# Attention with FP4-scaled weights on one core: where the weight loads stand in SyncE's queue, and where GpSimd's weight steps stand in a slot

## The reference

```
x = x + layernorm(attention(layernorm(x)))     # 16 heads of 128
x = x + layernorm(ffn(layernorm(x)))           # 8 experts, top 2
attention: w = codes * repeat(scales, 32, axis=0)   for wq, wk, wv (256 x 2048) and wo (2048 x 256)
           q, k, v = x @ w + b ; softmax(q k^T / sqrt(128)) v ; @ wo + bo
ffn:       softmax router, top-2 experts, silu(x Wg) * (x Wu) @ Wd, combined
```

## Time and profile before

| | |
|---|---|
| median of 3 runs | 2091.43 us |
| the profiled execution's own time | 2085.26 us |
| its span in the profile | 2083.5 us |
| TensorE matmul busy | 1966.5 us (94%) |
| VectorE busy | 1750.0 us (84%) |
| GpSimd busy | 1525.5 us (73%) |
| ScalarE busy | 1417.0 us (68%) |
| attention, roughly | 30 to 1850 us of the span |

### The profile page before, as it was taken

One profiled execution on the slowest core, in us unless ns is written; L12 is line 12 of the kernel. 1 busy time (PEld: TensorE's weight loads), 2 busy tenths in 40 slices (PEclk: granted clock), 3 DMA queues, 4 the chain that ended last, 5 costly groups with the idle time before them and its releaser, 6 DMA issues.

```text
span 2083.5 us, 33186 instructions
## 1 busy us (share of the span) xinstructions
PE 1966.5 (94%) x10902; PEld 1697.1 (81%) x10902; DVE 1750.0 (84%) x2706; ACT 1417.0 (68%) x2686; POOL 1525.5 (73%) x1317
## 2 busy tenths in 40 slices
PE   6999999999999999999999999999999999976882
PEld 5888888888888888888888888888888888865772
DVE  7889889998989888988999898988898898976444
ACT  5777767776777767776777667776777667762444
POOL 2679778887778777977888777977787787973222
PEclk9999999999999999999999999999999999986996
DMA  4667757786767767775767666765677566842443
GB/s 103 158 154 185 177 143 175 176 184 149 169 163 182 164 146 171 176 166 134 167 156 175 151 152 156 179 158 138 161 175 165 137 157 147 205 107 75 131 127 104
DMA packets 238064, 322.66 MB, mean 155 GB/s; under 512 B 47686, under 2 KB 105798, under 8 KB 237894
## 3 DMA queue, kind: packets, MB, share of 16 engines
q1 hardware_dynamic: 234822, 312.15, 63.4%
q0 software_dynamic: 3072, 8.39, 1.3%
HBM read 35.68 MB, written 18.35 MB: 26 GB/s over the span
## 4 chain that ended last, share of the span: by engine, by line
PE 69%; SPq 10%; POOL 6%; ACT 4%; DVE 4%; issue 3%; DMA 2%; another core or an unknown queue 0%; POOLq 0%; ACTq 0%
PE ps_a L749 16%; PE ps_s L621 12%; PE ps_s L622 11%; PE ps_s L623 11%; SPq L395 9%; PE ps_a L750 8%; POOL pT_both L518 5%; PE ps_a L621 3%; PE ps_a L623 3%; PE ps_a L622 3%; ACT probs L1037 2%; DVE part_max L1393 1%; DMA pT<-probs 1%; ACT pT_both L1054 1%; POOL x_rows L594 1%
## 5 line engine op out<-in xcount | busy, mean ns | idle before, releaser
L518 POOL TENSOR_TENSOR pT_both<-pT,pT_both 128x512 fp32r<-128x512 f32 x1016 | 1289.3, 1298 | 342.2 <-ACT pT_both L1054 340.6
L749 PE MATMUL ps_a<-pT_both,v_both 128*128 128x512 f32 x2048 | 743.8, 397 | 1.2 <-POOL pT_both L518 1.2
L1037 ACT ACTIVATE probs<-ps_s,shift 128x1024 f32<-128x1024 f32 x512 | 565.9, 1108 | 259.2 <-DVE shift L1402 258.9
L1054 ACT ACTIVATE pT_both<-pT 128x512 fp32r<-128x512 f32 x1016 | 605.7, 629 | 189.2 <-DMA pT<-probs 157.9
L1418 DVE STREAM_TRANSPOSE probs<-probs 128x1024 f32<-128x1024 f32 x508 | 614.2, 1229 | 58.3 <-ACT probs L1037 57.7
L1393 DVE TENSOR_REDUCE part_max<-ps_s 128x1 f32<-128x1024 f32 x512 | 612.0, 1214 | 19.9 <-PE ps_s L623 18.4
L750 PE MATMUL ps_a<-pT_both,v_both 128*128 128x256 f32 x2048 | 573.9, 280 | 0.0
L749 PEld LDWEIGHTS ps_a<-pT_both,v_both 128*128 128x128 f32 x2048 | 385.3, 188 | 86.6 <-POOL pT_both L518 1.1
L621 PE MATMUL ps_s<-kT_hi,qT_hi 128*128 128x512 f32 x1024 | 406.3, 397 | 15.3 <-ACT probs L1037 12.1
L622 PE MATMUL ps_s<-kT_lo,qT_hi 128*128 128x512 f32 x1024 | 402.9, 393 | 0.0
L623 PE MATMUL ps_s<-kT_hi,qT_lo 128*128 128x512 f32 x1024 | 401.3, 392 | 0.0
(11 more groups left out here) (202 smaller groups left out, 2584.5 us busy)
## 6 DMA issues: line engine op xcount, KB each, us to landing
pT<-probs SPq DMA_DIRECT2D x2032, 128.0 KB, 2.3
x_rows<-zeros SPq DMA_DIRECT2D x46, 128.0 KB, 2.2
xg<-x_rows SPq DMA_DIRECT2D x46, 128.0 KB
y_rows<-y_sb SPq DMA_DIRECT2D x46, 128.0 KB
pT<-in_L_attn_x SPq DMA_DIRECT2D x4, 512.0 KB, 5.7
codes<-in_L_attn_wk_codes SPq DMA_DIRECT2D x16, 128.0 KB, 2.4
scales<-in_L_attn_wk_scales SPq DMA_DIRECT2D x64, 32.0 KB, 3.0
codes<-in_L_attn_wo_codes SPq DMA_DIRECT2D x16, 128.0 KB, 2.3
```

Source lines behind the costliest of these rows:

```text
L518: pool.tensor_tensor(pT_lo[:, p, :].rearrange("p (i n) -> p i n", i=Q4), pT[:, s % 2, g, :, t:t + 2, :].rearrange("p i t q -> p i (t q)"), ...
L749: nc.tensor.matmul(out_both, v_hi[:, h % 2, k, :], move, start=k == 0, stop=False)
L1037: nc.scalar.activation(out, src, ACT.Exp, bias=shift[:, s % SLOTS, r:r + 1], scale=SCALE, accum_out=sums[:, s % SLOTS, r, g:g + 1])\
L1054: nc.scalar.activation(pT_hi[:, p, :].rearrange("p (i n) -> p i n", i=Q4), pT[:, s % 2, g, :, t:t + 2, :].rearrange("p i t q -> p i (t q)" ...
```

## The change

On SyncE each load now stands behind `turn_blocks(n)` instead of ahead of it, and a head's four loads stand two slots apart: after the transfers of s = 0 (k of the next head), s = 2 (q of the next head), s = 4 (v of the head after next) and s = 6 (o of the next head). The first o load stands ahead of the loop. In head 14 the order is k, o, q at s = 0, 2, 4. On GpSimd the three weight steps are split into three functions and put between low parts of a slot: the first behind low part 4, the second behind low part 5, the third behind low part 6, in the slots s = 0 (o), 2 (k), 4 (q) and 6 (v). In slot 6 of head 14 they stand behind low parts 1, 2 and 3.

```diff
--- before.py
+++ after.py
@@ -394,33 +394,30 @@
                         dst = pT[32 * b:32 * (b + 1), s % 2, :, i, :, :].rearrange("p g t q -> p g (t q)")
                         sp.dma_start(dst, src[:, :, b, :]).then_inc(pT_loaded[s % 2], 16)
 
+            sp.wait_ge(w_ready["k"], 1)
+            load("o", 0)
             for n in range(HALVES):
                 h, s = divmod(n, NH)
-                more = h + 1 < H
-                if s == 0 and more:
-                    wait(sp, w_ready["q"], h + 1)
-                    if h == 0:
-                        sp.wait_ge(w_ready["k"], 1)
-                    load("k", h + 1)
-                if n == 0:
-                    wait(sp, w_ready["k"], 2)
-                    load("o", 0)
-                if s == 1 and h > 0 and more:
-                    wait(sp, w_ready["k"], h + 2)
-                    load("o", h)
-                if s == 2 and h == H - 2:
-                    wait(sp, w_ready["o"], h + 1)
-                    load("o", h + 1)
-                if s == 2 and h + 2 < H:
-                    wait(sp, w_ready["o"], h + 1)
-                    load("v", h + 2)
-                if s == 4 and more:
-                    wait(sp, w_ready["o"], h + 1 if h + 2 < H else H)
-                    if h + 2 < H:
-                        wait(sp, w_ready["v"], h + 3)
-                    load("q", h + 1)
                 if n != LAST:
                     turn_blocks(n)
+                if s == 0 and h + 1 < H:
+                    wait(sp, w_ready["o"], h + 1)
+                    load("k", h + 1)
+                if s == 2 and h + 2 < H:
+                    wait(sp, w_ready["k"], h + 2)
+                    load("q", h + 1)
+                if s == 2 and h + 2 == H:
+                    wait(sp, w_ready["k"], h + 2)
+                    load("o", h + 1)
+                if s == 4 and h + 2 < H:
+                    wait(sp, w_ready["q"], h + 2)
+                    load("v", h + 2)
+                if s == 4 and h + 2 == H:
+                    wait(sp, w_ready["o"], h + 2)
+                    load("q", h + 1)
+                if s == 6 and h + 2 < H:
+                    wait(sp, w_ready["v"], h + 3)
+                    load("o", h + 1)
                 if HALVES - NH + 2 <= n < HALVES - NH + 2 + NCH:
                     g = n - (HALVES - NH + 2)
                     rows = slice(g * TPC, (g + 1) * TPC)
@@ -489,7 +486,7 @@
             pool.tensor_tensor(wr_both[:, :, 1, :], wr_raw[:, :, :], full(wr_both[:, :, 0, :]), ALU.subtract)\
                 .then_inc(sm["wr_lo_done"], 1)
 
-            def weights(k, h, codes=codes, scales=scales):
+            def weights_hi(k, h, codes=codes, scales=scales):
 
                 wait(pool, w_loaded[k], 16 * (NG + 1) * (max(h, 1) + 1 if k == "v" else h + 1))
                 if k == "o":
@@ -501,13 +498,20 @@
                     wait(pool, "k_ready", 2 * h)
                 else:
                     wait(pool, "v_ready", VU * (h // 2))
-                hi, lo = w_of(w_hi, k, h), w_of(w_lo, k, h)
-                pool.tensor_tensor(hi, codes[:, :, :], scales[:, :, :], ALU.mult).then_inc(w_hi_done[k], 1)
+                pool.tensor_tensor(w_of(w_hi, k, h), codes[:, :, :], scales[:, :, :], ALU.mult)\
+                    .then_inc(w_hi_done[k], 1)
+
+            def weights_scaled(k, h, codes=codes, scales=scales):
+
                 wait(pool, w_hi_done[k], h + 1)
                 pool.tensor_tensor(codes[:, :, :], codes[:, :, :], scales[:, :, :], ALU.mult)\
                     .then_inc(w_scaled[k], 1)
+
+            def weights_lo(k, h, codes=codes):
+
                 wait(pool, w_scaled[k], h + 1)
-                pool.tensor_tensor(lo, codes[:, :, :], full(hi), ALU.subtract).then_inc(w_ready[k], 1)
+                pool.tensor_tensor(w_of(w_lo, k, h), codes[:, :, :], full(w_of(w_hi, k, h)), ALU.subtract)\
+                    .then_inc(w_ready[k], 1)
 
             def probs_lo(w, p):
                 if not live(w) or w == LAST:
@@ -527,9 +531,13 @@
                 for t in range(RH * s, RH * (s + 1)):
                     pool.tensor_tensor(acc[:, t, :], acc[:, t, :], vb_sum[:, :], ALU.add).then_inc(sm["vb_added"], 1)
 
-            weights("k", 0)
+            weights_hi("k", 0)
+            weights_scaled("k", 0)
+            weights_lo("k", 0)
             for k, h in (("q", 0), ("v", 0), ("v", 1)):
-                weights(k, h, first_codes[f"{k}{h}"], first_scales[f"{k}{h}"])
+                weights_hi(k, h, first_codes[f"{k}{h}"], first_scales[f"{k}{h}"])
+                weights_scaled(k, h, first_codes[f"{k}{h}"], first_scales[f"{k}{h}"])
+                weights_lo(k, h, first_codes[f"{k}{h}"])
 
             pool.memset(zeros[:, :], 0.0).then_inc(sm["zeros_set"], 1)
 
@@ -549,18 +557,19 @@
 
             for n in range(HALVES + 2):
                 h, s = divmod(n, NH)
-                if s == 1 and h + 1 < H:
-                    weights("k", h + 1)
-                if s == 2 and h < H - 1:
-                    weights("o", h)
-                if s == 4 and h + 2 < H:
-                    weights("v", h + 2)
-                if s == 4 and h + 2 == H:
-                    weights("o", h + 1)
-                if s == 6 and h + 1 < H:
-                    weights("q", h + 1)
+                if h < H - 2:
+                    due = {0: ("o", h), 2: ("k", h + 1), 4: ("q", h + 1), 6: ("v", h + 2)}.get(s)
+                else:
+                    due = {0: ("o", h), 2: ("k", h + 1), 4: ("o", h + 1), 6: ("q", h + 1)}.get(s) if h == H - 2 else None
+                at = 1 if s == 6 and h == H - 2 else 4
                 for p in range(PAIRS_KT):
                     probs_lo(n - 2, p)
+                    if due and p == at:
+                        weights_hi(*due)
+                    if due and p == at + 1:
+                        weights_scaled(*due)
+                    if due and p == at + 2:
+                        weights_lo(*due)
                     if p == PAIRS_KT - 1 and h == H - 1:
                         add_bias(s)
```

## The result

The changed kernel took 2108.48 us, median of 6 runs (2105.93 to 2113.2); the kernel before, run beside it, 2092.19 us, median of 6 (2088.51 to 2094.27). The ratio is 1.0079 with a 95% interval of 1.0069 to 1.0090. So the change costs 16.3 us. The forecast had the direction and the mechanism, but 8.5 us of cost; 2108.48 lies just above its range. The profiled execution took 2106.0 us with a span of 2104.3, against 2085.26 and 2083.5 before.

What follows compares the result with a forecast made beforehand. Attention was taken to run at TensorE's pace. New stalls of 18.2 us less 8.0 of old ones gave +10.2, rounded to 8.5: 2091.4 + 8.5 = 2099.9, say 2100 us; eight times in ten 2089 to 2108.

Steps and rivals of the forecast that it cites:

- Step 1: Odd head's start: three weight steps (2.2 us) make SyncE's transfers 2.0 us late; chunk 72's high part still just in time.
- the limit: Latest start of a chunk's first high part without stalling TensorE: 5.4 us after the scores two chunks on start.
- Step 2: SyncE, odd chunks: a 2.6 us load ahead of their transfers makes chunk 73's high part 0.6 us late.
- the two special slots: Slots with another limit: 5.1 us with the bias step between high parts, about 5.7 with the fourth unit behind a bias product.
- Step 3: GpSimd's o-load wait (2.09 us) and early k and o steps go; chunk 74 still 0.8 us late, before 1.1.
- Step 4: Odd heads, even chunk to even chunk: loop of 26.3 us against TensorE's 25.2; lateness grows to 2.0, 2.3 us lost a head.
- the zeros' share: Heads 1, 3 and 5: a 0.59 us transfer of zeros per chunk raises the loss from 2.3 to 3.0 us a head.
- At no cost: even heads: Even heads lose nothing: value projections lengthen slots; units at s = 0 and 1 give 2.9 us more than an odd head's.
- Rounding 10.2 down to 8.5: Whole-kernel sum: net loss of 10.2 us cut to 8.5, partly because TensorE's stalls let SyncE and GpSimd catch up.
- No change: Rival, 18%: new lateness refills the old odd-head stalls to the same size, about 1.1 us a head; 2089 to 2095.
- Faster: Rival, 13%: GpSimd absorbs the steps, transfers take 10.2 us and odd-head stalls go; 2083 to 2087.
- Much slower: Rival, 9%: second stalls on `oT_lo` add 0.9 us per odd head, dragging issues the rest; 7 x 1.6 more, 2111.

Runs made afterwards that it cites:

- e: Changed kernel with each weight's three steps ahead of the first low part one slot later, loads as changed; 2061.47 us, 0.9974 of the kernel before.
- h: Changed kernel with the steps behind low parts 2, 3, 4 instead of 4, 5, 6, loads as changed; 0.9999 of the kernel before.
- i: Changed kernel with one more 128x256 multiplication on GpSimd (0.74 us, result unused) ahead of each set of weight steps; 1.0237 of the kernel before.
- a: Changed kernel with the weight steps put back ahead of low part 0 in the same slots, loads as changed; 1.0347 of the kernel before.
- b: Changed kernel with the loads put back ahead of the transfers of their slot, steps as changed; 1.0335 of the kernel before.
- c: Changed kernel with loads ahead of transfers and steps ahead of low parts, loads still two slots apart; 2060.5 us, 0.9963 of the kernel before.
- after_again: The changed kernel unaltered, run once more on another chip; 2083.82 us, 1.0073 of the kernel before.

## Why the prediction was right in kind and wrong in size

**Step 1, steps inside the slot: right on the start, wrong on "just in time".** It said that chunk 72's transfers start 7.4 us ahead of chunk 74's scores. They start at 1071.1, the scores at 1078.63: 7.5, against 9.4 before. But its high part was to be 0.2 us inside the limit and came 0.7 outside it, since these 16 transfers took 11.9 us and not 10.8. The mean over chunks 8 to 119 was 10.7: the price was right, its spread of 10.2 to 11.9 decides single chunks.

**Step 2, load behind the transfers: right in place, harmless by itself.** Issues stand back to back behind each load, and chunk 73's transfers start 2.7 us after chunk 72's last issue. By the limit of 5.4 us (5.1 and 5.7 in the two special slots), 22 of the 29 late high parts in heads 1 to 14 belong to odd chunks, the ones behind a load. Yet e has the same loads and a single late one: the steps use up the margin, and then the load puts the odd chunk over it. The prediction had named the Trainium skill, "DMA: Bandwidth & Descriptors", section "Issuing engines are not separate DMA queues", by which initiating a DMA is usually small beside it. The trace doesn't agree: a group of 16 issues took 10.2 to 11.9 us of SyncE in these rows and its data was there some 1.8 us later, and the five issues of a load do delay the transfers behind them.

**Step 3, what goes: right.** GpSimd's wait for scales fell from 16.5 and 10.3 us (o, k) to 0.3 in all, and the old stall in head 9 was filled again, as said (0.92 us idle before, 1.28 after): that saving bought nothing.

**Step 4, the two-slot loop: right.** e, h and i take away, shorten and lengthen just this loop by 2.2, 0.7 and 0.74 us, and the time follows. In head 9 the low parts of chunk 74 took 12.92 us with their steps (12.9 in the sum) and the whole loop from chunk 74's transfers to those of 76 27.5 us (26.3; the transfers took 11.9, not 10.8). The odd heads' stalls are 18.4 us where the step's sum had 18.2 (4 x 2.3 + 3 x 3.0); 10.0 more than before, where it had 10.2. That closeness is luck in good part. Heads 1, 3 and 5 stall 1.96, 2.05 and 2.20 us, 2.8 less than the sum's 9.0, and heads 7, 9, 11 and 13 3.15, 4.41, 2.57 and 2.06, 3.0 more than its 9.2: the zeros' share isn't seen, and head 9, the worked example, lost 4.4 us for 2.3.

**"At no cost: even heads": this step failed.** I gave an even head 2.9 us a slot for its value units. Those stand in the first slots only; from s = 3 on its slots last 12.6 to 12.9 us as an odd head's do. The rows of chunk 21 show the same stall for the same reason: 2.3 us of room, 3.3 us of new lateness. The even heads went from 0.9 to 5.4 us of stalls, head 14 from 3.3 to 4.5, and head 0 lost 0.7: 6.4 us costed at nothing. The row that misled me was one busy share over 113 us: 113.00 of 113 says that nothing is late, not how much room is left. After the change the same stretch, head 10, still reads 113.00, while heads 2 and 4 idle 0.7 us each in slot s = 7. The prediction also didn't have the new wait on `kT_lo` at a head's first chunk, 5 waits and 2.9 us, part of the odd heads' and of the even heads' figures.

**Rounding 10.2 down to 8.5: this step failed too.** Stalls should have let SyncE and GpSimd catch up; the odd heads' 10.0 show no such thing. With the 10.2 left alone the forecast would have been 2101.6, with the 6.4 also, 2108.0; measured 2108.48. The last agreement has luck in it too: the stalls are counted in one execution, whose span grew by 20.8 us where the medians grew by 16.3.

**The rivals.** No change and faster are out. "Faster" hung on GpSimd absorbing the steps; i shows that it doesn't behind low part 4, and e that it does in front of low part 0. "Much slower" was near in size (2111) for another reason: waits on `oT_lo` rose from 2 to 4, but from 1.5 to 1.6 us only. And by the Trainium skill, "Perfetto Trace Analysis", section "Identifying the Most-Contended Engine", weight loads at 85% would have meant free room on TensorE. The trace doesn't agree: late exponentials were paid for, 28.3 us of stalls at an unchanged 81% of the span.

## What to carry to other kernels

On an engine that works in order, ask of each place in the loop what is released behind it: the same 2.2 us of steps cost about 20 us between low parts whose end refills a buffer, and nothing in front of them, in the wait for that buffer's next contents. A load in front of transfers that have room to spare is harmless, and the same load makes them late once something else has taken the room. Whoever undoes half of a change must see that the other half doesn't move its wait onto the same loop, as a and b did; the clean undoing was one slot further on. A stretch that shows full busy time has no known slack until the latest producer in its tightest slot has been read.

## What the runs showed that I had not expected

- A kernel faster than both: both edits put ahead (c, 0.9963), or the steps put in odd slots (e, 0.9974). In both head 14's stall on the bias product, 3.8 and 4.2 us, is the largest left.
- The cost is steep once the loop is longer than TensorE's two slots: 0.74 us in it cost some 34 us over the kernel (i against the change), and 2.2 us taken out gave 20 (the change against e, 1.0073 to 0.9974 of 2067).
- Three chips ran the kernel before in 2066 to 2068 us, the chip of the result in 2092, with ratios of the change of 1.0073 and 1.0079. The difference lies behind attention: from head 15's last scores to the end the changed kernel took 272.4 us on that chip and 249.4 in after_again, while those scores started at 1831.9 and 1833.1 us. Why isn't shown.
